# Bias network on one core: third layer in rounds of four steps, and one first-layer read in eight moved from VectorE to ScalarE

## The reference

```python
pos = grid_q[:, :, None, :] - grid_kv[:, None, :, :]      # (16, 1024, 64, 2)
bias = jnp.sign(pos) * jnp.log1p(jnp.abs(pos))
bias = jax.nn.relu(bias @ cpb_w1 + cpb_b1)                # 2 -> 64
bias = jax.nn.relu(bias @ cpb_w2 + cpb_b2)                # 64 -> 64
bias = (bias @ cpb_w3 + cpb_b3)                           # 64 -> 1
sim = jnp.einsum('bhid,bhjd->bhij', qh, kh) + bias
```

## Time and profile before

| | us |
|---|---|
| median of 3 runs | 1541.29 (1540.26 to 1541.89) |
| profiled execution, its own time | 1542.36 |
| its span, first to last instruction | 1540.2 |
| around the span (own time less span) | 2.2 |
| bias network, first L633 copy to the sixteenth | 156.9 to 980.4 |

### The profile page before, as it was taken

The page is one execution under the profiler, slowest core; times in us unless marked ns, Lnnn a source line. Parts: engine busy times, 40 slices in busy tenths (PEclk is TensorE's granted clock), DMA queues, the critical chain, the costliest instruction groups (busy, mean ns, idle before and its releaser), DMA issues.

```text
span 1540.2 us, 32924 instructions
## 1 busy us (share of the span) xinstructions
PE 1441.7 (94%) x12718; PEld 634.1 (41%) x12718; DVE 1098.4 (71%) x1788; ACT 960.3 (62%) x1169; POOL 512.1 (33%) x571
## 2 busy tenths in 40 slices
PE   3179999999999999999999999979999899999998
PEld 1132222222222222222222222454445588888885
DVE  6867777777777777777777777751003899999995
ACT  2546666666666666666666666433120599999995
POOL 5232222222222222222222222230000177777773
PEclk8569999999999999999999999999999999999999
DMA  1130000000000000000000000000001622222211
GB/s 63 46 106 2 1 2 1 1 1 1 1 2 1 1 1 1 1 2 1 2 1 1 2 1 1 1 1 0 0 0 51 223 60 65 63 59 54 54 27 54
DMA packets 16152, 37.00 MB, mean 24 GB/s; under 512 B 4170, under 2 KB 7626, under 8 KB 15917
## 3 DMA queue, kind: packets, MB, share of 16 engines
q1 hardware_dynamic: 16032, 35.46, 7.9%
q10 hardware_dynamic: 12, 0.01, 0.0%
HBM read 24.57 MB, written 10.89 MB: 23 GB/s over the span
## 4 chain that ended last, share of the span: by engine, by line
PE 81%; DVE 12%; issue 3%; ACT 1%; POOL 1%; DMA 1%; SPq 0%; DVEq 0%; ACTq 0%; POOLq 0%
PE ps L832 31%; PE ps L840 16%; PE ps L824 9%; DVE aneg L714 4%; PE ps L996 4%; PE ps L1004 4%; PE ps L945 4%; PE ps L955 4%; PE ps L988 2%; DVE conv L577 2%; PE ps L979 1%; DVE big L717 1%; PE ps L932 1%; PE ps L967 1%; PE ps L1054 1%
## 5 line engine op out<-in xcount | busy, mean ns | idle before, releaser
L621 DVE TENSOR_SCALAR big<-ps 128x512 f32<-128x512 f32 x1032 | 644.5, 687 | 238.7 <-PE ps L824 238.7
L440 ACT ACTIVATE big<-ps,vec 128x1024 f32<-128x1024 f32 x514 | 563.6, 1115 | 321.7 <-PE ps L832 321.7
L832 PE MATMUL ps<-big,w 64*64 64x512 f32 x4112 | 549.1, 604 | 0.0
L335 POOL TENSOR_TENSOR mv<-sx,sy 128x1024 bf16<-128x1024 bf16 x130 | 248.4, 1911 | 644.4 <-PE ps L824 643.7
L840 PE MATMUL ps<-big,w3s 128*32 128x512 f32 x2048 | 272.8, 605 | 0.0
L832 PEld LDWEIGHTS ps<-big,w 64*64 64x64 f32 x4112 | 133.1, 133 | 310.0 <-DVE big L621 216.0
L376 POOL TENSOR_TENSOR big<-BT,big 128x512 f16<-128x512 f32 x129 | 150.4, 1166 | 249.8 <-DVE big L717 249.8
L824 PE MATMUL ps<-mv,wl 60*64 60x512 bf16 x2064 | 209.3, 391 | 1.9 <-ACT vs L435 1.1
L824 PEld LDWEIGHTS ps<-mv,wl 60*64 60x64 bf16 x2064 | 62.0, 105 | 282.3 <-DVE big L621 280.9
L714 DVE TENSOR_REDUCE aneg<-ps 128x1 f32<-128x1024 f32 x131 | 158.3, 1209 | 5.6 <-PE ps L988 5.4
L495 ACT ACTIVATE big<-ps,aneg 128x1024 f32<-128x1024 f32 x130 | 149.1, 1147 | 5.7 <-DVE aneg L714 5.1
(11 more groups left out here) (128 smaller groups left out, 949.0 us busy)
## 6 DMA issues: line engine op xcount, KB each, us to landing
h1h<-q_d SPq DMA_DIRECT2D x64, 128.0 KB, 2.9
h1l<-k_d SPq DMA_DIRECT2D x64, 128.0 KB, 3.1
q_d<-XN SPq DMA_DIRECT2D x8, 512.0 KB, 2.6
k_d<-XN SPq DMA_DIRECT2D x8, 512.0 KB, 2.6
X<-in_x SPq DMA_DIRECT2D x2, 1024.0 KB, 6.3
out<-X SPq DMA_DIRECT2D x8, 256.0 KB, 2.0
m<-grid_d SPq DMA_DIRECT2D x1, 1024.0 KB, 4.7
m<-in_m1T SPq DMA_DIRECT2D x1, 1024.0 KB, 5.9
```

The lines of the kernel that those rows point to most:

```text
L335: pool.tensor_tensor(mv[i][:, :].rearrange("p (a b) -> p a b", a=H), sx[:, g, jj, :].unsqueeze(1).to_broadcast(shape), sy[:, g, jj, :].uns ...
L440: act.activation(h2[m % HRING], z2[m % 2], ACT.Relu, bias=v("cb2")).then_inc(h2_ready, 1)
L621: dve.tensor_scalar(h1[m % HRING][:, HALF * a:HALF * (a + 1)], z1[n % 3], 0.0, None, ALU.max).then_inc(h1_ready, 1)
L832: last = pe.matmul(z2[m % 2][CH * a:CH * (a + 1), HALF * r:HALF * (r + 1)], w2[CH * r:CH * (r + 1), :], h1[m % HRING][CH * r:CH * (r + 1), ...
```

## The change

Layer three is issued once in `BURST` = 4 positions, for four steps in one go (twice four matmuls), after the `layer1` of that position. `h2` gets eight buffers for four. The layer-two and layer-one look-ahead stay at two and four steps. TensorE's order becomes L2(2) L1(4) L2(3) L1(5) L2(4) L1(6) L2(5) L1(7) L3(0,1) L3(2,3) | L2(6) L1(8) and so on. Half 1 of every step with m % 4 == 3 is read by ACT (`relu1b`, 128 x 512) behind `relu2(m - 2)`, under a semaphore of its own, `h1b_ready`. DVE reads the other seven halves of four steps.

```diff
-HRING = 4
+HRING, H2RING, BURST = 4, 8, 4
...
-        h2 = [big[:, i, :] for i in range(HRING)]
+        h2 = [big[:, i + i // 4 * 4, :] for i in range(H2RING)]
...
+            def relu1b(m):
+                act.activation(h1[m % HRING][:, HALF:N], z1[(2 * (m % PAIRS) + 1) % 3], ACT.Relu).then_inc(h1b_ready, 1)
...
             for g in range(G):
-                for m in range(AHEADQ, PAIRS + AHEADQ):
-                    act.wait_ge(z2_ready, PAIRS * g + m + 1)
-                    act.wait_ge(l3_done, PAIRS // 2 * g + m // 2)
+                for i in range(PAIRS):
+                    m = PAIRS * g + i + AHEADQ
+                    act.wait_ge(z2_ready, m + 1)
+                    if m >= H2RING:
+                        act.wait_ge(l3_done, m // BURST - 1)
                     relu2(m)
+                    if i % BURST == BURST - 1:
+                        act.wait_ge(z1_ready, m + 3)
+                        relu1b(m + 2)
...
             def relu1(m):
-                for a in range(2):
+                for a in range(1 if m % BURST == BURST - 1 else 2):
...
-                dve.wait_ge(l3_done, PAIRS // 2 * g + PAIRS // 2 + 1)
+                dve.wait_ge(l3_done, PAIRS // BURST * (g + 1))
...
+            def by_dve(m):
+                return 2 * (m + 1) - (m + 1) // BURST
+            def by_act(m):
+                return (m + 1) // BURST
...
             for g in range(G):
                 for i in range(PAIRS):
-                    m = i + AHEADQ
-                    pe.wait_ge(h1_ready, 2 * PAIRS * g + 2 * m + 2)
-                    pe.wait_ge(h2_ready, PAIRS * g + m - 1)
+                    m = PAIRS * g + i + AHEADQ
+                    pe.wait_ge(h1_ready, by_dve(m))
+                    if m % BURST == BURST - 1:
+                        pe.wait_ge(h1b_ready, by_act(m))
+                    pe.wait_ge(h2_ready, m - 1)
                     layer2(m)
-                    pe.wait_ge(h1_ready, 2 * PAIRS * g + 2 * m + (4 if i + AHEAD1 == PAIRS else 3))
+                    if i + AHEAD1 == PAIRS:
+                        pe.wait_ge(h1_ready, by_dve(m + 1))
+                        pe.wait_ge(h1b_ready, by_act(m + 1))
+                    else:
+                        pe.wait_ge(h1_ready, by_dve(m) + 1)
                     layer1(i + AHEAD1, g)
-                    if i % 2 == 1:
-                        pe.wait_ge(h2_ready, PAIRS * g + i + 1)
-                        if i == 1:
+                    if i % BURST == BURST - 1:
+                        pe.wait_ge(h2_ready, m - 1)
+                        if i == BURST - 1:
                             pe.wait_ge(bias_saved, g + 1)
-                        layer3(i - 1)
+                        for n in range(i - BURST + 1, i, 2):
+                            last = layer3(n)
+                        last.then_inc(l3_done, 1)
```

More of the change, by code:

```diff
@@ L175, in build @@
         q_copied, qk_ready = sem("q_copied"), sem("qk_ready")
-        mv_ready, z1_ready, h1_ready, z2_ready, h2_ready, l3_done = (
-            sem(x) for x in ("mv_ready", "z1_ready", "h1_ready", "z2_ready", "h2_ready", "l3_done"))
+        mv_ready, z1_ready, h1_ready, h1b_ready, z2_ready, h2_ready, l3_done = (
+            sem(x) for x in ("mv_ready", "z1_ready", "h1_ready", "h1b_ready", "z2_ready", "h2_ready", "l3_done"))
         bias_saved, w3_ready = sem("bias_saved"), sem("w3_ready")
@@ L439, in relu2 @@
             def relu2(m):
-                act.activation(h2[m % HRING], z2[m % 2], ACT.Relu, bias=v("cb2")).then_inc(h2_ready, 1)
-            act.sem_inc(l3_done, 1)
+                act.activation(h2[m % H2RING], z2[m % 2], ACT.Relu, bias=v("cb2")).then_inc(h2_ready, 1)
+            def relu1b(m):
+                act.activation(h1[m % HRING][:, HALF:N], z1[(2 * (m % PAIRS) + 1) % 3], ACT.Relu).then_inc(h1b_ready, 1)
             for m in range(AHEADQ):
@@ L445, in _ @@
                 relu2(m)
+                if m + 2 == AHEAD1 - 1:
+                    act.wait_ge(z1_ready, AHEAD1)
+                    relu1b(AHEAD1 - 1)
             for g in range(G):
-                for m in range(AHEADQ, PAIRS + AHEADQ):
-                    act.wait_ge(z2_ready, PAIRS * g + m + 1)
-                    act.wait_ge(l3_done, PAIRS // 2 * g + m // 2)
+                for i in range(PAIRS):
[3 more added lines that the diff above has]
+                        act.wait_ge(l3_done, m // BURST - 1)
                     relu2(m)
+                    if i % BURST == BURST - 1:
+                        act.wait_ge(z1_ready, m + 3)
+                        relu1b(m + 2)
             for u in range(G + 2):
@@ L840, in layer3 @@
                     last = pe.matmul(zb[32 * k:32 * (k + 1), :], w3s[:, a:a + 32],
-                                     h2[(m + k // 2) % HRING][:, HALF * (k % 2):HALF * (k % 2 + 1)],
+                                     h2[(m + k // 2) % H2RING][:, HALF * (k % 2):HALF * (k % 2 + 1)],
                                      start=(m == 0), stop=(m == PAIRS - 2))
-                last.then_inc(l3_done, 1)
+                return last
             pe.wait_ge(ld_w2, 16 * 3)
@@ L854, in _ @@
             for m in range(AHEADQ):
-                pe.wait_ge(h1_ready, 2 * m + 2)
+                pe.wait_ge(h1_ready, by_dve(m))
                 layer2(m)
-                pe.wait_ge(h1_ready, 2 * m + 3)
+                pe.wait_ge(h1_ready, by_dve(m) + 1)
                 layer1(m + 2, 0)
@@ L860, in _ @@
                 for i in range(PAIRS):
-                    m = i + AHEADQ
-                    pe.wait_ge(h1_ready, 2 * PAIRS * g + 2 * m + 2)
-                    pe.wait_ge(h2_ready, PAIRS * g + m - 1)
-                    layer2(m)
-                    pe.wait_ge(h1_ready, 2 * PAIRS * g + 2 * m + (4 if i + AHEAD1 == PAIRS else 3))
+                    m = PAIRS * g + i + AHEADQ
+                    pe.wait_ge(h1_ready, by_dve(m))
+                    if m % BURST == BURST - 1:
+                        pe.wait_ge(h1b_ready, by_act(m))
+                    pe.wait_ge(h2_ready, m - 1)
+                    layer2(m)
+                    if i + AHEAD1 == PAIRS:
+                        pe.wait_ge(h1_ready, by_dve(m + 1))
+                        pe.wait_ge(h1b_ready, by_act(m + 1))
+                    else:
+                        pe.wait_ge(h1_ready, by_dve(m) + 1)
                     layer1(i + AHEAD1, g)
-                    if i % 2 == 1:
-                        pe.wait_ge(h2_ready, PAIRS * g + i + 1)
-                        if i == 1:
+                    if i % BURST == BURST - 1:
+                        pe.wait_ge(h2_ready, m - 1)
+                        if i == BURST - 1:
                             pe.wait_ge(bias_saved, g + 1)
-                        layer3(i - 1)
+                        for n in range(i - BURST + 1, i, 2):
+                            last = layer3(n)
+                        last.then_inc(l3_done, 1)
             def sims(u):
@@ L899, in values @@
                 last.then_inc(o_ready, 1)
-            pe.wait_ge(h1_ready, 2 * (PAIRS * G + AHEAD1))
+            pe.wait_ge(h1_ready, by_dve(PAIRS * G + AHEAD1 - 1))
+            pe.wait_ge(h1b_ready, by_act(PAIRS * G + AHEAD1 - 1))
             pe.wait_ge(h2_ready, PAIRS * G + AHEADQ)
```

## The result

The changed kernel takes 1559.9 us (median of 4 runs, 1557.7 to 1560.8) against 1541.6 before: a ratio of 1.0117, with a 95% interval of 1.0100 to 1.0135. It is slower by 18 us (15.4 to 20.8 by the interval). The forecast was 1562, in a range of 1549 to 1577.

A forecast was written before the change was run, and what follows sets the result against it. TensorE was taken as the bound, with the chain that matters through DVE's reads. A round of 7.02 us against 6.86 for two old periods, 128 x 0.16 = 20.5 us more, gives 1562, range 1549 to 1577.

The forecast's parts named there:

- the sign that the prediction named: TensorE's step from L1(5) to L2(4) should be 0.60 us, not 0.21; without it the prediction is wrong.
- Saved changes of shape: Fewer switches on TensorE between layer three and the other layers save 0.29 us a round, 37 us in all.
- the lower of the two bounds: A layer three's second pass directly before another layer three: between 0.43 and 0.55 us, taken as 0.43.
- The stalls that replace them: L2(4) waits 0.39 and L2(5) 0.10 us for DVE's second reads, L1(5) 0.10; two late weight loads cost 0.04 each.
- ACT's half read: ACT's read of step 7's half 1 ends by 5.95 us, needed at 7.23: no cost, no gain.
- Rival 1: L2 needn't wait for DVE's second read, only TensorE's tiling-mode drain counts: round 6.65, 27 us less, 1514; chance 0.08.
- Rival 2: Same terms, but the L2 stalls come to about 0.41 us a round: no change, 1541; chance 0.05.
- Rival 3: DVE's read rate bounds the kernel and ACT's read relieves it: round 6.77, 12 us less, 1530; chance 0.03.
- Rival 4: Slower still: further releases (1575), L3 behind L3 paying 0.55 (1577), or a lower clock (1605); chance 0.10 for all three.
- further release: Extra semaphore instructions at the two stalled layer twos cost 0.05 us each: 0.10 a round, 13 us.
- the clock's price: TensorE's granted clock at 0.95 on the round's 6.37 us of work: 0.33 more a round, 43 us, 1605.

The follow-up runs named there:

- e4: Kernel before with layer two one position later; layer three still after every second position, eight h2 buffers, DVE reads all halves: 1542.9 us, ratio 1.0011.
- e3: Changed kernel with layer two one position later and DVE reading all halves, layer three still in rounds of four: 1521.0 us, ratio 0.9878.
- e5: Changed kernel with DVE's read of half 1 cut to 256 of 512 columns, TensorE's and ACT's work the same: 1524.3 us, ratio 0.9898.
- e6: Changed kernel with DVE reading all halves and the layer threes of seven rounds in eight left out: 1382.0 us, ratio 0.8970.
- e1: Changed kernel with ACT's half read taken back, so DVE reads all eight halves of a round: 1558.5 us, ratio 1.0119.
- e2: Changed kernel with layer three back after every second position, ACT's half read and eight h2 buffers kept: 1540.2 us, ratio 0.9999.
- e7: Changed kernel with layer two one position later, ACT's half read kept but behind the relu2 three steps earlier: 1520.6 us, ratio 0.9866.

## Why the prediction was right

The mechanism was the one forecast: the step from L1(5) to L2(4), the sign that the prediction named, is 0.60.

- **Saved changes of shape (0.29 a round).** As forecast. The merged layer threes take 404.87 to 406.72 = 1.85 (forecast 1.86). Two layer threes in a row have four passes. With 0.45 for the first and 0.55 for the last, as before, 1.85 leaves 0.85 for the two in the middle, and the weight loads there stand 0.42 apart (405.33, 405.75). So the middle passes take 0.42 to 0.43, the lower of the two bounds. e4 against e3 gives 0.31 for the whole term.
- **The stalls that replace them.** Shown by the starts in the profile after, by the dose in e5, by e6, where nothing else is left, and by e3, where they are gone. L2(4) waited 0.39 forecast and 0.38 measured; L2(5) 0.10 and 0.08 (403.63 less 403.33 + 0.22).
- **The size, 20.5 us against 16.6 by the pace and 18 by the runs.** A round grew by 0.13 and not by 0.16. No single term is off by more than 0.01: L1(5) came 0.01 later than laid out, and L2(4) to L1(6), L1(6) to L2(5), L1(7) to L3 and the two layer threes each took 0.01 less. Together they make 0.03 of a round, 128 x 0.03 = 4 us. That is within the 0.05 to 0.1 that the prediction allowed for its terms. The step L1 to L3 is 0.34 behind an L1 that had waited for DVE (in the kernel before and in e3, 405.22 to 405.56) and 0.33 here (404.54 to 404.87), behind one that had hardly waited; why, no run shows. The 1.4 us between pace and runs lie within the interval of 15.4 to 20.8.
- **ACT's half read.** At no cost and no gain, as forecast (e1, e2). It took 0.59 us, shorter than the 0.62 to 0.69 assumed, and ended 5.75 us after L1(4), 1.5 us before it was needed.
- **Rival 1 (only the drain counts)** would be 1514. It describes e3 quite well, at 1521: take the wait for the second read away, and the round is 6.70 where the rival had 6.65. The difference is DVE's rate, 1.21 for 1.18 twice. So the rival had the size of the saving right, and was wrong in that the order of the change has the wait.
- **Rival 2 (a draw)** needed the stalls of layer two, with their late weight loads, at 0.41 a round. They are 0.38 + 0.08 and some 0.08 for the loads.
- **Rival 3 (DVE's rate relieved by ACT)** fell with e1, e2 and e7. Half of it holds in e3: with the second read out of the way, two of the three steps between layer ones are DVE's two reads, 1.21. The half that ACT takes isn't among the reads that set them.
- **Rival 4.** No further release was seen at the two stalled layer twos: 0.05 from the end of the read to the start, as before. TensorE's granted clock was 1.00 (the level of 2.4 GHz) in each of nine stretches from 100 to 990 us, with PE busy for 97.2 to 97.4% of each. (The 6.37 us of work in the clock's price should be 7.02 - 0.67 = 6.35; the 0.33 stays.) One of these windows of the changed kernel, in the columns of the earlier trace rows:

```profile
400.00:500.00 100.00, 97.38 (x920) 25.94 (x912) 63.96 (x102) 69.92 (x72) 26.61 (x14) 1.00 0.01 1
```

## What to carry to other kernels

Work that is moved out from between two dependent steps takes its cover with it. Before bunching, lay the new order out on paper with the latencies of the chain (here L1, two reads, L2: 1.78 us), and see what now stands next to its producer. If something does, lengthen the lead of the producer in the same edit: here one position more turned 18 us lost into 20 us won (e7_lead3_act, 0.9866). Taking load from an engine with idle time gained nothing here, as the piece that was taken was one that nothing waited for; making the piece shorter that was waited for gained as much as the piece got shorter (e5_short).

## What was not expected of the hardware

That busy time hides stalls was known, but not how much: the kernel before counts as 100% busy in the network with a stall of 0.10 us in each period of 3.43, and the changed one as 97.4% with some 8% of each round lost (0.10 + 0.38 + 0.08, of 6.99). Starts in the rounds that were read (between 400 and 409 us, at a granted clock of 1.00) repeat from round to round and from kernel to kernel within 0.01 us. So the round worked out from the trace of the kernel before came out 0.03 us too long in 7. The later ones, which could also use the trace of the changed kernel, were within 0.03 us of what was measured (e3, e4, e5, e6).
